# A fused convolution, attention and expert kernel: the second norm's inverse deviations and its normalising step move by one unit

## The reference, cut to what matters

```
t = t + attn(ln_t(t))        # 6 heads of 16, causal softmax, projection Wp, bias bp
t = t + ffn(ln_t(t))         # 4 experts, the 2 best by a softmax gate, gelu, hidden 384
ln_t(v) = (v - mean(v)) / sqrt(var(v) + 1e-5)      # over the 96 channels of a token
```

## Time and profile before

| quantity | value |
|---|---|
| median of three runs | 429.06 us (427.37 to 430.52) |
| the profiled execution's own time | 431.65 us |
| its span (the part with work on the engines) | 429.7 us |
| PE busy | 404.0 us, 94% of the span |
| DVE busy | 248.3 us, 58% |
| ACT busy | 267.1 us, 62% |
| POOL busy | 147.6 us, 34% |
| mean granted TensorE clock | 0.987 of full speed |

### The profile page before, as it was taken

How to read it: one execution, slowest core, us unless ns; L and a number is a source line. 1 busy time by engine, 2 the same in 40 slices (tenths; PEclk the granted TensorE clock), 3 DMA queues, 4 the chain that set the end, 5 groups by cost and what they waited for, 6 DMA issues and landing times.

```text
span 429.7 us, 10320 instructions
## 1 busy us (share of the span) xinstructions
PE 404.0 (94%) x3024; PEld 332.1 (77%) x3024; DVE 248.3 (58%) x867; ACT 267.1 (62%) x766; POOL 147.6 (34%) x314
## 2 busy tenths in 40 slices
PE   7999998887999899989998999899989998999996
PEld 4988984555588788868886888789777887787786
DVE  1576774475328753866386548645864585367425
ACT  3566652465486658665865686567747764877380
POOL 6000002366305631563155315532642254236200
PEclk9899999998899999999999999999999999999999
DMA  7700000310111012101200220021002100210000
GB/s 177 177 0 0 0 2 19 83 29 2 43 36 36 2 46 53 30 0 50 55 23 0 54 55 21 0 61 49 18 0 64 46 0 8 76 27 3 7 13 20
DMA packets 16472, 14.87 MB, mean 35 GB/s; under 512 B 7586, under 2 KB 13588, under 8 KB 16452
## 3 DMA queue, kind: packets, MB, share of 16 engines
q1 hardware_dynamic: 14644, 13.74, 12.4%
q10 hardware_dynamic: 1616, 0.74, 0.7%
q0 software_dynamic: 192, 0.15, 0.2%
HBM read 3.80 MB, written 1.57 MB: 12 GB/s over the span
## 4 chain that ended last, share of the span: by engine, by line
PE 72%; DVE 9%; issue 7%; POOL 6%; ACT 3%; DMA 1%; ACTq 1%; SPq 1%; POOLq 0%; DVEq 0%
PE F L1126 14%; PE T L1084 6%; PE A L1105 5%; PE F L1142 5%; PE F L1146 4%; PE F L1143 4%; PE F L957 3%; POOL p_sb L453 3%; PE S L1068 3%; PE S L1070 2%; ACT p_sb L598 2%; PE F L967 2%; DVE xh L770 2%; PE F L968 2%; PE S L1073 2%
## 5 line engine op out<-in xcount | busy, mean ns | idle before, releaser
L453 POOL TENSOR_SCALAR p_sb<-p_sb,rden 128x128 f32<-128x128 f32 (+1 forms) x192 | 79.5, 429 | 115.3 <-DVE rden L798 113.1
L1126 PE MATMUL F<-w_sb,hid 128*128 128x96 f32 x768 | 98.8, 272 | 0.0
L1126 PEld LDWEIGHTS F<-w_sb,hid 128*128 128x128 f32 x768 | 96.1, 192 | 0.0
L598 ACT ACTIVATE p_sb<-S,nmax 128x128 f32<-128x128 f32 (+1 forms) x192 | 78.9, 424 | 11.4 <-DVE nmax L792 11.4
L792 DVE TENSOR_REDUCE nmax<-S 128x2 f32<-128x512 f32 (+1 forms) x80 | 50.6, 632 | 51.5 <-PE S L1073 51.2
L1084 PE MATMUL T<-id_sb,p_sb 128*128 128x128 f32 x288 | 48.1, 286 | 12.3 <-POOL p_sb L453 10.4
L502 ACT COPY pt_sb<-T 128x512 f32<-128x512 f32 (+1 forms) x48 | 26.5, 551 | 44.6 <-PE T L1084 44.6
L644 ACT ACTIVATE hid<-F,b_sb 128x512 f32<-128x512 f32 x72 | 49.4, 689 | 7.0 <-PE F L1146 6.3
L1084 PEld LDWEIGHTS T<-id_sb,p_sb 128*128 128x128 f32 x288 | 31.5, 144 | 21.9 <-POOL p_sb L453 17.7
L598 ACT ACTIVATION_READ_ACCUMULATOR p_sb<-S,nmax 128x1 f32 x192 | 39.7, 207 | 0.0
L1068 PE MATMUL S<-k_bd,q_st 96*128 96x384 f32 (+2 forms) x96 | 38.1, 404 | 1.5 <-ACT p_sb L598 1.1
(11 more groups left out here) (151 smaller groups left out, 789.3 us busy)
## 6 DMA issues: line engine op xcount, KB each, us to landing
k_bd<-k_cur SPq DMA_DIRECT2D x93, 32.0 KB, 2.0
q_st<-q_cur SPq DMA_DIRECT2D x28, 96.0 KB, 2.3
k_bd<-k_cur SPq DMA_DIRECT2D x93, 16.0 KB, 1.8
t_st<-t_cm SPq DMA_DIRECT2D x7, 192.0 KB, 2.5
out_y<-y_sb SPq DMA_DIRECT2D x7, 192.0 KB, 1.9
x_pad<-in_x SPq DMA_DIRECT2D x2, 612.0 KB, 7.4
w_sb<-in_w SPq DMA_DIRECT2D x1, 576.0 KB
hid<-in_w SPq DMA_DIRECT2D x1, 576.0 KB, 6.8
```

What stands on the lines that cost most here:

```text
L453: last = nc.gpsimd.tensor_scalar(p, p, rden[:, u % 3, i:i + 1], 1.0, ALU.mult, ALU.mult)
L598: last = nc.scalar.activation(p_sb[:, u % 3, i * nk:(i + 1) * nk], S[u % 2][:, i * nk:(i + 1) * nk], ACT.Exp, bias=nmax[:, u % 3, i:i + 1] ...
L1126: last = mm(dst[:, e * C:(e + 1) * C], hid[:, c, s * TT:(s + 1) * TT], w2_sb[:, c], start=False, stop=(c == NCH - 1), skip_group_check=True)
```

## The change

On POOL, `rstd2` of tile s moves from step `TILE_END[s] + 1` to `TILE_END[s] + 2`, but at the latest to step 9. So `rstd2` of tile 0 comes behind the scaling of unit 5 (before: of unit 4), that of tile 1 behind the scaling of unit 8 (before: of unit 7). That of tile 2 moves from step 8 to step 9, but POOL has no scaling left at step 9, so its place in the stream is the same: behind the scaling of unit 9.

On DVE, `normalize2` of tile s moves from step `TILE_END[s] + 2` to `TILE_END[s] + 3`: tile 0 from step 4 to step 5, tile 1 from step 7 to step 8. Tile 2 would fall on step 10, which the loop doesn't have; it is issued right behind the loop, which is the same place in the stream as before, since it was the last thing of step 9. Number and shape of all instructions stay as they are; no DMA is touched.

```diff
@@ POOL, body @@
                     for s in range(SPB - 1):
-                        if j == TILE_END[s] + 1:
+
+                        if j == min(TILE_END[s] + 2, NU - 1):
                             rstd2(n, s)
                 rstd2(n, SPB - 1)
                 keep_t1(n, first)
@@ DVE, body @@
                     for s in range(SPB - 1):
                         if j == TILE_END[s] + 1:
                             attn_residual(n, s, first)
-                        if j == TILE_END[s] + 2:
+                        if j == TILE_END[s] + 3:
                             normalize2(n, s)
+                normalize2(n, SPB - 2)
                 if not first:
                     for s in range(sum(FILL[:-1]) // NCH, sum(FILL) // NCH):
                         combine(n - 1, s, second)
```

## The result

The changed kernel takes 431.44 us (median of 20 runs), the kernel before 428.56 us (median of 20 runs). The ratio is 1.0062, with a 95% interval of 1.0043 to 1.0081: 1.8 to 3.5 us more. The forecast was 431.0 us, +2.0 us. The profiled execution took 433.3 us with a span of 431.5 us. The ratio leaves out one execution of the changed kernel, 556.61 us at a mean granted clock of 0.643; the kernel before had one like it (557.2 us, 0.643) in the experiments.

The account below looks back on a forecast made before the run. The bound was PE's 1.09 us stall per block at unit 8's transposes, through DVE's row maximum and POOL's scalings. Six blocks of 0.32 us, +0.2 and -0.14 gave +2.0 us: 431.0 us from 429.06, range 427.0 to 433.5.

Parts of the forecast that it names:

- Tile 0 on POOL: POOL's inverse deviation of tile 0 behind unit 5's scaling: costs nothing, with a cover of 0.05 us at unit 6.
- Tile 0 on DVE: DVE's normalising of tile 0, now at step 5's end, puts unit 8's row maximum off by 0.25 us.
- Unit 8's scaling 0.26 us earlier: On POOL, unit 8's scaling starts at 314.27 instead of 314.53; its transposes start at 315.28 instead of 315.54.
- The stall goes to unit 9: PE's stall moves from unit 8's to unit 9's transposes, behind POOL's inverse deviation of tile 1; 0.32 us later per block.
- rival 3: DVE's normalising of tile 1 stretches unit 9's POOL scaling by 0.32 us in seven blocks: 433.2 us; chance 0.08.
- Block 7, +0.2 us: Last block: 0.09 us of slack at tile 3's projection leaves some 0.2 of the 0.32 us loss.
- Block 0, -0.14 us: First block: stall of 0.59 us before unit 5 removed, then unit 9's loss; middle between -0.59 and +0.32 us.
- rival 2: Block 0 keeps PE's clock because less idle time precedes it; some 3 us saved, 428.0 us; chance 0.12.
- rival 4: PE's clock falls to 0.50 around units 8 and 9, about 3 us in each of six blocks: 449 us; chance 0.04.
- rival 1: PE doesn't wait for unit 9's scaling; the 0.26 us gained at unit 8 passes on: 427.5 us; chance 0.12.

Follow-up runs that it names:

- DVE's half alone: Against the kernel before, only DVE's normalising of tile 0 moves to step 5, POOL's stream unchanged: 41.89 us a block, ratio 1.0063.

## Why the prediction was right

- **Tile 0 on POOL, nothing:** right, 0.03 us a block (41.92 against 41.89).
- **Tile 0 on DVE, +0.25 us in front of unit 8's row maximum:** right. The row maximum is put off by 0.23 us, DVE's half alone costs 0.22 us a block, twice costs twice.
- **Unit 8's scaling 0.26 us earlier:** it came 0.33 us earlier (315.15 - 0.95 = 314.20 against 314.53). Its transposes came 0.24 us earlier and not through the mechanism I named: DVE's copy of unit 7 ended at 316.10, just behind the scaling's 316.09, and released them 0.15 us later. I had left that copy out. It made no difference, since unit 9 sets the end.
- **The stall goes to unit 9, +0.32 us:** +0.28 us at its transposes, +0.31 us a block. The scaling held 0.06 us more than the row I took.
- **Port sharing (rival 3):** a stretch was there, 0.06 instead of 0.32 us; that a port causes it is not shown. The rows that I read as "no stretch" have the normalising begin inside the scaling. The trace of the kernel before also held the other case, in block 0: the first norm's normalising on DVE began 0.06 us ahead of a scaling on POOL, which took 0.99 us. All engines' timeline, cut to the two:

```profile
94.28 1.35 DVE L770 TENSOR_SCALAR xh<-t,mv,rs 128x96 f32<-128x96 f32 x4
...
94.34 0.99 POOL L453 TENSOR_SCALAR p_sb<-p_sb,rden 128x256 f32<-128x256 f32 x2
```

- **Block 7, +0.2 us:** mis-sized. From block 6's to block 7's transposes of the second norm it is 39.70 in both profiles of the change and 39.41 and 39.42 in those of before, so +0.29 us. Unit 9's transposes are already later by that much, and the slack of 0.09 us that I read off did not help: in the changed kernel DVE still took up tile 3's projection 0.05 us behind its end (402.88 + 0.43 = 403.31, then 403.36), so 0.05 us of it was the way from PE to DVE.
- **Block 0, -0.14 us:** a middle between two bounds, and not shown. Its stall of 0.59 us at unit 5 is gone, but unit 6's scaling, now behind the inverse deviation, makes a new one, as PE's timeline of block 0 of the changed kernel shows:

```profile
98.28 0.55 PE L1086 MATMUL T<-id_sb,p_sb 128*128 128x128 f32 x3
...
100.46 0.55 PE L1086 MATMUL T<-id_sb,p_sb 128*128 128x128 f32 x3 [1.03 <-POOL p_sb L453]
```

  The clock moved block 0 by 2.7 us between two executions of the kernel before, near the 3 us at which rival 2 priced it, and that hides a tenth of a us. No profile of the change kept a clock of 1.00 through block 0; the nearest that did, with tile 1 normalised at step 9, took 40.09 us against 40.16 us, and its other blocks are 0.08 us shorter than those of the change. So the term is more likely near zero than a gain.
- **The clock falling in every block (rival 4), and the gain that passes on (rival 1):** neither was seen. The gain does pass on once the inverse deviation leaves unit 9's way too.

The sum of what was measured, 6 x 0.31 + 0.29 = 2.2 us without block 0, stands beside the forecast of +2.0 and the measured 1.8 to 3.5 us. The mechanism was right in its main terms; that the total came so near is in part luck, since block 0's term was a guess between two bounds. The medians lie 2.9 us apart. Late keys add 0.36 us in one of the two profiles of the change; the rest of that difference the profiles don't place.

## What to carry to other kernels

Taking a short instruction out from in front of one link of a chain gains nothing if it lands in front of the next link of the same chain; it has to go behind the last one. When an off-path step is moved, look at both ends of the move on each engine: here the DVE half left a place where its time turned into waiting and took one where every instruction counts in full. Compare such changes by the length of the repeating block in the profile, which repeats within 0.1 us where whole runs scatter by 3 to 4.

## What the runs showed of the hardware

- One kernel, two executions: behind equal stalls of 1.43 and 1.42 us TensorE's granted clock fell to 0.50 for some 7 us in block 0 in one and stayed at 1.00 in the other; block 0 took 42.90 and 40.16 us. In the first it had also fallen to about half between 12 and 16 us, and the kernel's start took 1.6 us longer.
- A POOL scaling of two 128x256 pieces took 0.99 instead of 0.93 us when a DVE normalising of 128x96 began 0.05 or 0.06 us ahead of it; where the normalising began inside the scaling it took 0.94 us in the same profile and in the first one of the kernel before.
- A transfer of the keys came late in one block of one profile (3.60 us in the chain, the block 0.36 us longer), and not in the next profile of the same kernel; with tile 0 normalised twice one came late in one block as well (3.65 us, 0.44 us longer).
